# A decoder layer on one core: causal scores in three fills instead of four, bf16 matmuls ahead of f32 ones, and the setup block dissolved into the schedule

## The reference

```
x = x + local_attn(layernorm(x))            # keys within 3 tokens; Wq, Wk, Wv, Wo with biases
x = x + cross_attn(layernorm(x), ctx)       # 120 context keys; Wq, Wk, Wv, Wo with biases
y = layernorm(x)
y = y + causal_attn(rmsnorm(y)*n1_w)        # mask: a query sees keys up to itself; no biases
out = y + silu-MLP(rmsnorm(y)*n2_w) * factor   # 256 -> 1024 -> 256; factor from a gate of 8 logits
attn(q, k, v) = softmax(q k^T / 4) v        # 16 heads of 16
```

## Time and profile before

| | us |
|---|---|
| median of 3 runs | 4187.93 (4185.14 to 4190.39) |
| the profiled execution | 4194.42 |
| its span, first to last instruction | 4192.7 |
| PE busy | 3875.9 (92%) |
| PE weight loads, beside the matmuls | 3152.4 (75%) |
| DVE / POOL / ACT busy | 2506.0 / 2490.8 / 1857.2 (60% / 59% / 44%) |
| granted TensorE clock, mean | 0.976 |

### The profile page before, as it was taken

The page is one execution under the profiler, slowest core; times in us unless marked ns, Lnnn a source line. Parts: engine busy times, 40 slices in busy tenths (PEclk is TensorE's granted clock), DMA queues, the critical chain, the costliest instruction groups (busy, mean ns, idle before and its releaser), DMA issues.

```text
span 4192.7 us, 96887 instructions
## 1 busy us (share of the span) xinstructions
PE 3875.9 (92%) x40328; PEld 3152.4 (75%) x40328; DVE 2506.0 (60%) x4820; ACT 1857.2 (44%) x3393; POOL 2490.8 (59%) x3156
## 2 busy tenths in 40 slices
PE   4799999999999999999999999999999999999997
PEld 3577777777777777777777777777777777777775
DVE  4666665565665665665665665665665665665642
ACT  1344444444444444444444444444444444444442
POOL 4766665665665665666655666655656656656621
PEclk9799999999999999999999999999999999999998
DMA  4101111111111111111111111111111111111100
GB/s 142 61 36 61 47 50 64 44 54 63 41 55 64 39 58 64 39 58 64 39 58 64 39 58 64 39 58 62 41 58 64 37 59 53 46 62 49 48 7 8
DMA packets 87142, 221.54 MB, mean 53 GB/s; under 512 B 8316, under 2 KB 53688, under 8 KB 70328
## 3 DMA queue, kind: packets, MB, share of 16 engines
q1 hardware_dynamic: 86712, 215.34, 14.5%
HBM read 164.92 MB, written 50.39 MB: 51 GB/s over the span
## 4 chain that ended last, share of the span: by engine, by line
PE 77%; ACT 9%; POOL 6%; DVE 4%; DMA 2%; issue 2%; SPq 0%; POOLq 0%; DVEq 0%
PE ps L822 10%; PE ps L813 10%; PE ps L794 8%; PE ps L693 8%; PE ps L658 7%; PE ps L674 7%; PE ps L758 7%; PE ps L728 7%; ACT prob L902 6%; PE ps L680 4%; POOL chunks L1016 3%; PE ps L771 2%; PE ps L640 2%; ACT held L879 2%; DMA k_windows<-passed_k 1%
## 5 line engine op out<-in xcount | busy, mean ns | idle before, releaser
L1021 POOL TENSOR_TENSOR chunks<-v_windows,xT 128x560 f32<-128x560 f32 (+1 forms) x384 | 869.0, 2288 | 424.7 <-DVE xT L1114 422.1
L1016 POOL TENSOR_TENSOR chunks<-rest,k_windows 128x512 f32<-128x512 f32 (+1 forms) x384 | 549.4, 1452 | 519.2 <-DMA k_windows<-passed_k 463.2
L902 ACT ACTIVATE prob<-ps 120x1024 f32<-120x1024 f32 (+1 forms) x512 | 620.0, 1240 | 436.7 <-PE ps L736 436.7
L1137 DVE TENSOR_REDUCE nmax_pair<-ps 128x16 f32<-128x1920 f32 (+2 forms) x320 | 712.9, 2228 | 126.2 <-PE ps L703 108.0
L1032 POOL TENSOR_SCALAR_AFFINE_SELECT prob<-prob 128x512 f32<-128x512 f32 x512 | 313.4, 636 | 383.4 <-ACT prob L902 383.4
L813 PE MATMUL ps<-xT,w_up 128*128 128x256 f32 x2048 | 481.1, 383 | 12.2 <-ACT xT L863 11.6
L1094 DVE TENSOR_REDUCE xT<-chunks 128x32 f32<-128x512 f32 (+1 forms) x384 | 296.0, 772 | 311.2 <-POOL chunks L1016 311.1
L758 PE MATMUL ps<-prob,va 120*32 120x256 f32 (+2 forms) x6144 | 337.7, 371 | 143.0 <-ACT prob L902 139.5
L822 PE MATMUL ps<-w_down,held 128*128 128x256 f32 x2048 | 455.1, 380 | 4.2 <-DVE held L1183 4.2
L1094 DVE TENSOR_REDUCE held<-chunks 128x80 f32<-128x560 f32 (+1 forms) x384 | 296.2, 771 | 271.0 <-POOL chunks L1021 269.2
L728 PE MATMUL ps<-held 32*120 32x256 f32 (+2 forms) x6144 | 389.2, 367 | 51.6 <-ACT prob L902 45.7
(11 more groups left out here) (147 smaller groups left out, 6724.8 us busy)
## 6 DMA issues: line engine op xcount, KB each, us to landing
k_windows<-passed_k SPq DMA_DIRECT2D x64, 1024.0 KB, 4.9
v_windows<-passed_v SPq DMA_DIRECT2D x64, 1024.0 KB, 7.0
x<-in_x SPq DMA_DIRECT2D x64, 256.0 KB, 2.9
passed_k<-rest SPq DMA_DIRECT2D x64, 256.0 KB, 2.0
passed_v<-held SPq DMA_DIRECT2D x64, 256.0 KB, 2.1
out<-x SPq DMA_DIRECT2D x64, 256.0 KB, 2.2
y<-in_ctx SPq DMA_DIRECT2D x64, 120.0 KB, 2.8
w_up<-in_up SPq DMA_DIRECT2D x1, 1024.0 KB
```

Of the source, the lines that this page charges most:

```text
L902: last = nc.scalar.activation(dst[0:keys], ps[0:keys, first:first + 4, n * T:n * T + dst.shape[2]], ACT.Exp, scale=SCALE)
L1016: last = nc.gpsimd.tensor_tensor(chunk_of(c).rearrange("p (j d) -> p j d", d=D), q_row, window("k", (b + first) * D, (D, n), (1, D)), ALU. ...
L1021: last = nc.gpsimd.tensor_tensor(chunk_of(c).rearrange("p (h i j) -> p h i j", i=HD, j=WINDOW), window("v", b * D + first * HD, (HD, n), ( ...
L1137: nc.vector.tensor_reduce(dst, src, AX_X, ALU.max, negate=True).then_inc(emptied[b], 1)
```

## The change

Four things change.

1. The causal scores are three units. The first two hold two groups each for keys 0 to 127 (256 queries, the shape of the cross units), the third all four groups for keys 128 to 255 (128 queries). A third unit is held back by the plan until the first two stand. ACT's exponential is two activations of 128x1024 for units 0 and 1, and four of 128x512 for unit 2. POOL still masks eight times 128x512 a sequence: two in units 0 and 1, four in unit 2.
2. In every `scores` unit the bf16 matmuls that carry the maximum come first and open the accumulation; the f32 ones follow.
3. The setup block is gone. `setup_parts` adds steps of the schedule: five groups of weights by first use, the zeros (now two DMAs over one scratch tensor), and `derive` steps: the cross and causal weights are turned on ACT (16 instructions each layer, the scaling by n1 within), the rest of the scaling, the biases, `pick` and the two tables on DVE and PE. The staging place of the turned weights is `prob` instead of `held`. Waits on them are made once per engine.
4. Some busy times in the plan's table are new (`round_max` 0.52 to 0.6, `scores` 1.1 to 1.04 for cross, `values` 1.76 to 1.66 and 2.6 to 2.54, `weigh` 1.2 to 1.5).

The diff, cut to its core:

```diff
 def score_units(layer):
-    return [(0, 1), (2, 3)] if layer == CROSS else [(0,), (1,), (2,), (3,)]
+    fills = [((0, 0), (1, 0)), ((2, 0), (3, 0))]
+    return fills if layer == CROSS else fills + [tuple((g, 1) for g in range(4))]
...
+LOADS = (("local_k", "local_v", "local_bk", "local_bv"), ("local_q", "local_o", "local_bq", "local_bo"),
+         ("cross_q", "cross_k", "cross_v", "cross_o", "cross_bv", "cross_bo"),
+         ("causal_q", "causal_k", "causal_v", "causal_o", "cross_bq", "cross_bk", "n1"),
+         ("up", "down", "gate", "n2"))
+def setup_parts():
...
+    loads = [part("weights", (n,), "SP", busy, [], lag=lag)
+             for n, (busy, lag) in enumerate(((2.0, 5.0), (2.0, 6.0), (3.0, 10.0), (4.5, 12.0), (5.5, 18.0)))]
+    part("zeros", (), "SP", 0.6, [], lag=2.5)
+    tables = part("derive", ("tables",), "PE", 1.0, [])
+    part("derive", ("tables",), "DVE", 1.4, [tables])
+    part("derive", ("pick",), "DVE", 0.9, [])
+    part("derive", ("bias",), "DVE", 4.6, [loads[3], ("derive", ("pick",), "DVE")])
+    part("derive", ("scale",), "DVE", 4.3, [loads[3], loads[4]])
+    part("derive", ("cross",), "ACT", 3.6, [loads[2]])
+    part("derive", ("causal",), "ACT", 3.6, [loads[3]])
...
-            for u, gs in enumerate(score_units(layer)):
+            held = []
+            for u, unit in enumerate(score_units(layer)):
                 step = ("scores", (layer, u))
-                a = part(*step, "PE", 1.1 if layer == CROSS else 0.82, [shifted],
-                         [("quad", step)] + [("prob", (layer, g)) for g in gs])
-                a = part(*step, "ACT", 1.9 if layer == CROSS else 1.36, [a], (), [("quad", step)])
+                first = [p for p in held if u == 2]
+                a = part(*step, "PE", 1.04, [shifted] + first[0::2],
+                         [("quad", step)] + [("prob", (layer, g)) for g, kb in unit if kb == 0])
+                held.append(a)
+                a = part(*step, "ACT", 1.9 if u < 2 else 2.3, [a] + first[1::2], (), [("quad", step)])
...
     elif name == "scores":                                     # on PE
-                        for n, g in enumerate(score_units(L)[u]):
-                            m, e = divmod(g, 2)
-                            for key0, keys, q0, qs, col in key_blocks(L, T, C):
-                                for r in range(4):
-                                    rows = slice(32 * r, 32 * r + 32)
-                                    nc.tensor.matmul(ps[0:keys, first + r, n * T + col:n * T + col + qs],
-                                                     kT[s][rows, m, key0:key0 + keys], qT[s][e][rows, m, q0:q0 + qs],
...
+                        for n, (g, kb) in enumerate(score_units(L)[u]):
+                            key0, keys, q0, qs, col = key_blocks(L, T, C)[kb]
+                            for r in range(4):
+                                rows = slice(32 * r, 32 * r + 32)
+                                nc.tensor.matmul(ps[0:keys, first + r, n * qs:(n + 1) * qs], pick[rows, g, 0:keys],
+                                                 nmaxT[s][rows, q0:q0 + qs], start=(n == 0), stop=False,
...
+                                last = nc.tensor.matmul(ps[0:keys, first + r, n * qs:(n + 1) * qs],
+                                                        kT[s][rows, m, key0:key0 + keys],
+                                                        qT[s][e][rows, m, q0:q0 + qs], start=False, stop=True,
...
-        with nc.Block() as block:                              # the whole setup block
...
+                    if name == "weights":                      # on SP
+                        n, = args
+                        for what in LOADS[n]:
...
+                    elif name == "zeros":
+                        sp.wait_ge(filled_ones, 1)
+                        for first in (0, T + HALO):
+                            dst = passed_on[:, first:first + HALO, :].rearrange("a r d -> r a d")
+                            src = zero_rows[0:HALO, :].unsqueeze(1).to_broadcast([HALO, 2 * LANES, D])
+                            sp.dma_start(dst, src).then_inc(zeroed, 16)
...
+                    if name == "derive":                       # on ACT
+                        what, = args
+                        n = 2 if what == "cross" else 3
+                        act.wait_ge(loaded[n], 16 * len(LOADS[n]))
...
+                                            last = nc.scalar.activation(dst[:, k, a, m], src[:, k, a, m],
+                                                                        ACT.Identity, scale=scale1[:, k:k + 1])
```

More of the change, by code:

```diff
@@ L77, in sequence_parts @@
 def sequence_parts(T, C):
     out = []
+    weights = [("weights", (n,), "SP") for n in range(len(LOADS))]
+    needs = {("project_rows", "k"): [weights[0]], ("project_rows", "v"): [weights[0]],
+             ("project_rows", "q"): [weights[1]], ("project_out", LOCAL): [weights[1]],
+             ("project_out", CROSS): [weights[2]], ("project_out", CAUSAL): [weights[3]],
+             ("fetch", "k"): [("zeros", (), "SP")], ("fetch", "v"): [("zeros", (), "SP")],
+             ("project", CROSS): [weights[2], ("derive", ("cross",), "ACT"), ("derive", ("bias",), "DVE")],
+             ("project", CAUSAL): [("derive", ("causal",), "ACT"), ("derive", ("scale",), "DVE"),
+                                   ("derive", ("bias",), "DVE")],
+             ("max", CROSS): [("derive", ("tables",), "DVE")], ("max", CAUSAL): [("derive", ("tables",), "DVE")],
+             ("gate", None): [("derive", ("scale",), "DVE")], ("up", 0): [("derive", ("scale",), "DVE")]}
@@ L81, in part @@
+    needs.update({("up", m): needs["up", 0] for m in range(1, 4)})
     def part(name, args, engine, busy, after, takes=(), gives=(), lag=None):
-        out.append(Part(name, args, engine, busy, LAG[engine] if lag is None else lag, tuple(after), tuple(takes),
+        first = engine in ("PE", "SP")
+        also = needs.get((name, args[0] if args else None), []) if first else []
+        out.append(Part(name, args, engine, busy, LAG[engine] if lag is None else lag, (*after, *also), tuple(takes),
@@ L221, in __init__ @@
         missing = {(n, i): len(p.after) for n in range(N) for i, p in enumerate(parts)}
+        todo = [(n, i) for n in range(N) for i in range(len(parts)) if n == 0 or i >= len(once)]
         ready = {e: [] for e in engines}
@@ L226, in offer @@
             ready[parts[i].engine].sort()
-        for n in range(N):
-            for i, p in enumerate(parts):
-                if not p.after:
-                    offer(n, i)
+        for n, i in todo:
+            if not parts[i].after:
+                offer(n, i)
         idle, events, now = set(engines), {}, 0.0
@@ L267, in __init__ @@
                     for j in followers[i]:
-                        missing[n, j] -= 1
-                        if not missing[n, j]:
-                            offer(n, j)
-        assert sum(map(len, self.order.values())) == N * len(parts)
+                        for m in range(N) if i < len(once) <= j else (n,):
+                            missing[m, j] -= 1
+                            if not missing[m, j]:
+                                offer(m, j)
+        assert sum(map(len, self.order.values())) == len(todo)
         self.lane = [self.slot["lane", n, ()] for n in range(N)]
@@ L402, in sem @@
             return sems[-1]
+        constants, filled_ones, zeroed = sem("constants"), sem("filled_ones"), sem("zeroed")
+        loaded = [sem(f"loaded{n}") for n in range(len(LOADS))]
+        derived = {what: sem(f"derived_{what}") for what in ("tables", "pick", "bias", "scale", "cross", "causal")}
+        tables_filled = sem("tables_filled")
         filled = [sem(f"filled{b}") for b in range(SINGLES + QUADS)]
@@ L445, in half_max, with once @@
             return nmax_parts[s][:].rearrange("p b (r x) -> p (b r) x", x=32)
+        def once(eng, known, what, signal, count):
+            if what not in known:
+                known.add(what)
+                eng.wait_ge(signal, count)
         def wait_taken(eng, name, n, *args):
@@ L651, in _ @@
                         w, = args
+                        n = 1 if w == "q" else 0
+                        once(pe, known, f"weights{n}", loaded[n], 16 * len(LOADS[n]))
                         wait_taken(pe, "turn", seq, LOCAL)
@@ L870, in _ @@
                         L, w = args
+                        once(act, known, "bias", derived["bias"], 1)
                         b = bank(name, seq, args)
@@ L1078, in _ @@
                         w, = args
+                        n = 1 if w == "q" else 0
+                        once(dve, known, f"weights{n}", loaded[n], 16 * len(LOADS[n]))
                         b = bank(name, seq, args)
```

310 lines of the change are left out of this document (164 added, 146 removed).

## The result

The changed kernel takes 4034.1 us (median of 4 runs, 4033.2 to 4037.7), the kernel before in the same job 4189.2 (4 runs): ratio 0.9632, 95% interval 0.9615 to 0.9648, 155 us less. The profiled execution of the changed kernel took 4037.7, its span 4035.9; 4192.7 before.

A forecast was written before the change was run, and what follows sets the result against it. PE was taken to set the pace at 63.29 us a sequence. From the profiled 4194.4: -107 over 58 sequences, -28 setup, +2 end, 4061; 6.5 less for the median, 4055. Own range 4015 to 4100; 8 in 10, 3965 to 4145.

The forecast's parts named there:

- Cross values' wait goes: PE's wait of 2.50 us for ACT's exponentials ahead of the cross values goes in all three sequences.
- New waits, 7.4 us in three sequences: PE's waits in the new three-sequence pattern sum to 7.4 us, 2.5 a sequence against 3.28 before.
- Dips: Low-clock stretches after PE's waits cost about 0.9 us a sequence before; 0.4 taken for the new kernel.
- Clean work, 58.55: PE's undisturbed work falls from 59.1 to 58.55 us a sequence through fewer divided stretches and bf16 first.
- 61.45: Forecast steady time a sequence on PE: 58.55 work, 2.5 waits, 0.4 dips; 1.84 us less than 63.29.
- The setup, 28: At the start, POOL's first window product comes near 34 us instead of 65; net gain 28 us, bounds 18 and 40.
- The end, 2 us later: The longer third causal unit, on ACT and in masks, delays the last sequences by some 2 us.
- The other side: Rival: work piles up on DVE and POOL, late masks double DVE waits, dips rise; 64.4 a sequence, 4227 us, chance 0.06.
- only the setup helps: Rival: new waits as long as the old with as many dips, 63.3 us a sequence; 4160 us, chance 0.17.
- the setup gains nothing: Rival: up and down weights in the DMA queue hold up later fetches too; 4083 us, chance 0.07.
- that of DVE's queue: Same rival as "The other side": DVE's third-sequence queue, deciding once waits pass 12 us in three sequences; chance 0.06.
- Waits nearly vanish: Rival: steps overlap more than the walk assumed, dips go too; 59.5 to 60 us a sequence, 3957 us, chance 0.20.

The follow-up runs named there:

- e4: The kernel before with only the plan's new cost numbers, still four causal units; 4192.4 us, ratio 0.9998.
- e8: The kernel before with one plan number changed, so cross values stand five steps behind their scores, four units kept; 4400.3 us, ratio 1.0486.
- e7: The kernel before with five useless float32 full-array products where TensorE waits ahead of the cross values; 4167.4 us, ratio 0.9943.
- e3: The changed kernel with float32 scores first in each unit, same plan; 4048.5 us, ratio to the kernel before 0.9656.
- e6: The kernel before with bfloat16 scores first in each of its four units, nothing else; 4163.4 us, ratio 0.9931.
- e1: The kernel before with only the setup block dissolved into steps, old scores and costs; 4179.1 us against 4192.5, ratio 0.9971.
- e5: The changed kernel with the fourth and fifth sequences' loads issued ahead of the last weights; 4032.7 us, ratio to the kernel before 0.9620.
- e12: e11 with DVE's scaling of the MLP and causal value weights moved behind three products of the second sequence's windows; 3953.3 us.
- e2: The kernel before, setup block kept, with three causal units, bfloat16 first and the new costs; 4054.0 us, ratio 0.9670.
- e11: e5 with ACT's exponential times in the plan set to 2.1 and 2.4 us instead of 1.9 and 2.3; 3953.4 us, ratio 0.9424.

## Why the prediction was right, and where it was not

The forecast was 4055, in its own range of 4015 to 4100; the time is 21 us under it, half a per cent. Point by point:

- **Cross values' wait goes.** Right: none in the list, and with its dips (2.50 + 0.85 us) it is the largest term. The three units are what moves the values back (e4), and moving them back with four units lost 202 us (e8); the prediction took the order from the pattern and couldn't test this.
- **New waits, 7.4 us in three sequences.** The places were right but for two, the sum somewhat high: 5.6 on the mean. The `max` behind the third unit waits 1.50 (1.7 said), `shift` 1.12 (1.4), `turn_out` 0.38 with 0.72 at the turn ahead (1.6), the second cross `max` 0.47 (0.4), `down` 0.52 (0.9). `up`'s 0.5 didn't come and the causal query projection waits 0.19 instead of 0.6; a wait of 0.54 at a cross key projection was not foretold.
- **Dips.** The 0.9 of before is confirmed (0.85 by e7), and so is it that they follow the idle time. The term of 0.4 was too high: cross values never took long again, and 4 of 126 stretches are under 1.00. Waits up to 1.5 us bring almost none.
- **Clean work, 58.55.** This was the term mis-sized the other way: 59.08 (60.95 less waits), against 59.16 before by the table (63.29 less 3.28 less 0.85). The scores gave what was said and more, 0.64: 0.34 for bfloat16 first, where I took 0.2, and 0.30 for the fills, where I had 0.25 + 0.1. But the MLP steps take 0.29 more, projections 0.12 and transposes 0.09, which I had at nothing. They are the same instructions in another order. Which neighbour costs them how much wasn't tried. The rule on tiling that the prediction weighed would by itself have put the order within a unit at nothing; e3 shows 0.07 a unit (0.34 in five), e6 0.05 (0.31 in six).
- **So 61.45 became 60.95** a sequence; 52 of them give 121.5 instead of 96.
- **The setup, 28.** The failed term: 13 us timed, 16.5 in the profile (e1). The first product was foretold to the quarter of a microsecond (34 for 34.24), and for its reason: it waits for the fetch, and 263 GB/s over the first 29 us make 7.6 MB, where the sum had 7.5 by then. But the sum took all the rest of the pipeline to move with it, less 3. It did not: PE was held 9.9 us by a context behind the weights, and half the lead was gone by the v products (31.1 us at the first key product, 15.0 at the first v product; 14.4 in e1). e5 gives 5 us of it back; e12 shows that moving the scaling does not give the rest, and no run shows what would.
- **The end, 2 us later.** Wrong in sign: from the 60th `down` to the end it takes 13.2 us less. The prediction counted no gain of pace there; e2 has 8.2 of it and e1 none. Why isn't shown.
- **A sum among the rivals.** "The other side" doubles two waits, +3 us in three sequences. That is 1 a sequence, where its sum has 2.3: with 1 it comes to 63.15 a sequence and about 4152 us, which isn't slower. Its chance was put on a time that its own mechanism doesn't give.

The setup was put 11.5 us too high. Against that stand 20 us from the pace (127 for 107: 121.5 in the 52, and 5.6 before them once the setup's 16.5 is taken off) and 15 from the end. So the total is nearer than its terms, and in part by luck. Of the rivals, "only the setup helps" is excluded by e2, "the setup gains nothing" by e1, and that of DVE's queue by its own measure: waits of 5.6 in three sequences, where it was to decide from 12. "Waits nearly vanish" didn't come, but e11 shows that it was to be had: 59.64 a sequence, 3953 us.

## What to carry to other kernels

Before moving a step away from a wait, read what the engine it waits for has queued next: if the next step needs the next item of that queue, the wait only changes its place, and can grow (e8). An idle gap on TensorE of some 2.5 us cost a third more than itself here (0.85 us on the mean), by the clock behind it; work of no use in its place was a gain (e7). And in a kernel ordered by a plan, try its costs against the trace after each change of the steps: here that was worth 79 us over the same kernel with the old ones (e5), half of what the change itself brought, though these two values were picked by the plan's count. An earlier first product isn't an earlier pipeline until the next waits are read too.

## What the runs showed of the hardware

- Full-array products of 2.40 us in the place of a 2.5 us wait kept the granted clock at 1.00 in all 126 stretches of 25 us (e7). Waits of 2.5 us were followed by long cross values in 27 of 52 cases; with waits of 1.5 us and less, 4 of 126 stretches were under 1.00 in the changed kernel and none in e2 and e11. Why one wait of 2.5 brings the low clock and the next, equal one doesn't stays open.
- Around a 3.2 us wait of e8 the granted clock was 0.81 over 9 us, and the transposes and the projection behind it took up to twice as long (`turn` 0.89 start to start for 0.49, the cross keys 1.69 for 0.89).
- A divided step that starts with the bfloat16 products (0.26 start to start) and ends with float32 takes 0.05 to 0.09 us less than the reverse, for the same products (e6: 1.03 for 0.98 in a causal unit; e3: 1.29 for 1.23 in a cross unit and 1.29 for 1.20 in the first two causal ones).
